# Cross attentions of a two-layer perceiver: the 257th probabilities sent through a DRAM row, transposes and copies two units at a time

## Chip, cores and metric

One core of one Trainium2 chip runs the whole program. The metric is the time of one execution on the device in microseconds. Engines run their own queues and meet at semaphores: PE (TensorE, matmuls; its weight loads, PEld, overlap them), DVE (VectorE), ACT (ScalarE), POOL (GpSimd), SP (SyncE, whose queue issues all the DMAs). PSUM has eight banks of 128 x 512 float32; only PE writes them by matmul, only DVE and ACT read them here.

## The reference, cut to what matters

64 sequences of 32 tokens of width 256 go through two layers. Each layer has a cross attention to a context of 257 positions per sequence, a self attention of its own kind, and a feed-forward part. The change touches only the two cross attentions, `_L0_xattn_ref` (4 key heads, with a mask and RMS norms) and the cross part of `_L1_xattn_ref` (8 key heads, LayerNorms):

```
q = norm(project(x)).reshape(16 heads, 128)
k = norm(ctx @ Wk)              # 257 positions, 4 or 8 key heads
v = ctx @ Wv
probs = softmax(q . k)          # 257 probabilities for each query row
out = (probs @ v) @ Wo
```

The kernel computes `probs @ v` as `(probs @ ctx) @ Wv`: first each query row's weighted sum of the 257 context rows, then the value projection of it.

## The kernel before

`cross_attention` runs once for each layer. A tile is four sequences (BT = 4 batches b = 0 to 3, 128 token rows), and there are 16 tiles. A batch has 32 tokens x 16 heads = 512 query rows, in four units (v = 0 to 3) of 128 rows each: `pr[:, v, :]` holds a unit's 128 x 257 scores and then probabilities, one query row to a partition.

Each engine walks the same schedule written out by hand: `tile` calls `slot(i, s, ...)` for s = 0 to 3. Slot s projects the keys of batch s and computes its scores, and handles batch s-1 (`back(i, s, 1, ...)`) and, in layer 0, the values of batch s-2. Work on the next tile's tokens and queries is spread over the slots: in slot 0 the tokens of tile i+1 are normalised, transposed on PE after the second key (L320) and their queries projected. `run` repeats `tile` in a loop; after the last tile, slots without keys drain what is left. Layer 1 takes the values of two batches together (`project_value_pair`, in slots 1 and 3).

PE's order in a slot: for g = 0 to 3 the key projection g (L345, two accumulating matmuls of 128x128 by 128x257, each run as two instructions) into one of two banks, then the transposition of unit g of batch s-1; in layer 1 key 4; then values (L391, or L403 in layer 1); the sum of the keys' squares over a head (L353); the scores of units 0 and 1 (L364); pieces of query or output work, with keys 5 to 7 of layer 1 among them; the scores of units 2 and 3; last, `weigh_context` for batch s-1 (L382), whose two halves go to banks PC0 and PC1.

`transpose_probs` transposes a unit's probabilities into bank PTb: positions 0 to 127 and 128 to 255 by two transposes (L373), and the 257th position by a third (L375), whose source is that one column broadcast over 128 columns; so its result holds, on every partition, the 128 rows' 257th probability. `copy_probs` on DVE (L861) copies the three blocks (128x384) into `pT[:, :, v*128:...]`. There is one bank PTb, so the transposes of unit v+1 wait for the copy of unit v (`pt_copied`), and each copy waits for its transposes (`pt_done`). `weigh_context` multiplies the first 256 context rows `cn` with `pT[:, 0:2]`, and DVE's `copy_weighed` (L869) adds the 257th position when it empties the bank: `pT[:, 2, :]` (the probabilities) times `cT[:, b, h, 256]` (that position's context value on this partition) plus the bank, into `pcT`.

In layer 0 ACT takes each key from its bank (L595) and squares it (L597). In layer 1 DVE takes it (`copy_key`, L826) and then ACT squares it (L591). The next key in that bank waits for the square (`k_sq`). ACT then makes the reciprocal root of the summed squares (L604, L606), DVE scales the scores into `pr` (`shift_scores`, L844 in layer 0, L836 in layer 1), ACT exponentiates (L611) and normalises (`norm_probs`, L617, signal `pn_done`), with `norm_probs` of unit 3 at the start of the next slot. `shift_scores` of unit v waits until the previous batch's unit v has been transposed, as it overwrites it.

DVE's order at a slot's start: (in slot 0) statistics of the next tokens, the reciprocal of unit 3's sum, `copy_weighed` of batch s-2's second half, then for each g `copy_key` g (layer 1) and `copy_probs` g; in slot 0 `norm_tokens` (L769) behind g = 0 and, in layer 1, `quantise_tokens` behind g = 2. `copy_weighed` of batch s-1's first half is the last thing in a slot.

SP loads the context of batch b (`load_context`, L294 and L296: cT 257 KB, cn 256 KB) for the next tile when `pcT` of this tile's batch b has been written.

Of the kernel before, what the change touches and what calls it, by code (L numbers as in the profile page):

```python
# [6 lines left out]
F32 = mybir.dt.float32  # L7
# [8 lines left out]
P = 128  # L16
H = 256
HC = H // P
# [77 lines left out]
def cross_attention(nc, d, X, Yc, ident, layer, tiles):  # L96
# [24 lines left out]
    with Part(nc) as ctx:  # L121
# [8 lines left out]

        wq = sb("wq", [P, HC, NH * HD])
# [42 lines left out]
        pT = sb("pT", [P, KC + 1, UNITS * P])  # L174
# [59 lines left out]
        pt_done = sig("probs_transposed", BT * UNITS)  # L234
        pt_copied = sig("pT_copied", BT * UNITS)
# [42 lines left out]
        def _(sp):  # L278
# [10 lines left out]
            for s in ctx_in:  # L289
                s.prime(sp)  # L290

# [6 lines left out]

            load_context(0, 0)
# [4 lines left out]
            with sp.Fori(1, tiles) as i:  # L304
                for b in range(BT):
                    load_context(i, b)
# [4 lines left out]
        def _(pe):  # L311
# [56 lines left out]
            def transpose_probs(t, b, v):  # L368
                u = UNITS * b + v
                pe.wait_ge(pn_done.sem, pn_done.now(t, u + 1))  # L370
                pe.wait_ge(pt_copied.sem, pt_copied.after(t, u))
                for c in range(KC):
                    pe.transpose(PTb[:, c * P:(c + 1) * P], pr[:, v, c * P:(c + 1) * P], ident[:])  # L373
                last = pr[:, v, LAST:SE].to_broadcast([P, P])
                pe.transpose(PTb[:, KC * P:(KC + 1) * P], last, ident[:]).then_inc(pt_done.sem, 1)  # L375

            def weigh_context(t, b):
                pe.wait_ge(pt_copied.sem, pt_copied.now(t, UNITS * (b + 1)))
# [99 lines left out]
            def slot(i, s, cur, prev, nxt):  # L478
                for g in range(4):
                    if cur:  # L480
                        project_key(i, s, g)
                    for t, b in back(i, s, 1, cur, prev):
                        transpose_probs(t, b, g)
                    if g == 1 and s == 0 and nxt:
                        if prev:
                            pe.wait_ge(pc_copied.sem, pc_copied.now(i - 1, HC * (BT - 1)))
                        transpose_tokens(i + 1)
# [230 lines left out]
        def _(dve):  # L718
# [110 lines left out]
            def shift_scores(t, b, v):  # L829
# [3 lines left out]
                dve.wait_ge(pt_done.sem, pt_done.after(t, u + 1 - UNITS))  # L833
# [22 lines left out]
            def copy_probs(t, b, v):  # L856
                dve.wait_ge(pt_done.sem, pt_done.now(t, UNITS * b + v + 1))
                if v == 0:
# [89 lines left out]
            def slot(i, s, cur, prev, nxt):  # L948
# [6 lines left out]
                for g in range(4):  # L955
                    if L1 and cur:
                        copy_key(i, s, g)
                    for t, b in back(i, s, 1, cur, prev):
                        copy_probs(t, b, g)
# [1768 lines left out]
```

## Time and profile before

| | |
|---|---|
| median of 3 runs | 4377.0 us (4372.99 to 4379.25) |
| profiled execution | 4376.91 us, its span 4375.1 us |
| instructions | 84534 |
| PE busy | 3906.8 us, 89% |
| PE weight loads busy | 2551.8 us, 58% |
| DVE busy | 2551.3 us, 58% |
| ACT busy | 1863.2 us, 43% |
| POOL busy | 216.3 us, 5% |

The cross attention of layer 0 lies roughly in the second to tenth of the page's 40 slices, that of layer 1 in slices 22 to 35. Matmuls are pipelined: the time of one (283 ns on average for a transpose) is longer than the distance from its start to the next one's start, so the distances between starts in the timeline tell what one costs. A line of the timeline merges equal instructions that follow each other (x4 is four). "[0.70 <-PE ...]" is the engine's idle time before the line and what ended it.

### The profile page before, as it was taken

What the parts mean: (1) busy time and instruction counts of PE and PEld (TensorE: products, weight loads), DVE (VectorE), ACT (ScalarE), POOL (GpSimd) and SP (SyncE); (2) the same over time, 40 slices, a digit from 0 to 9 for tenths busy, and PEclk for the clock granted to TensorE, in tenths of its full rate; (3) what the DMA queues carried; (4) which work ended last, traced back from release to release, by engine and by line L of the source; (5) the groups of instructions that cost most, each with busy time, mean ns of one, the idle gap of its engine ahead of it and who ended that gap; (6) DMA issues with size and microseconds to landing.
All of it is one profiled execution on the core that took longest, in us unless ns stands there. A gap on an engine that the chain in (4) does not pass through costs nothing. (4 is left out here: it accounts for less than half of the span.)

```text
span 4375.1 us, 84534 instructions
## 1 busy us (share of the span) xinstructions
PE 3906.8 (89%) x29984; PEld 2551.8 (58%) x29984; DVE 2551.3 (58%) x6013; ACT 1863.2 (43%) x5062; POOL 216.3 (5%) x164
## 2 busy tenths in 40 slices
PE   6999999999799985888874999999999999789798
PEld 3666666666433552555553666666666666579555
DVE  4565655555311445777764677776777667457521
ACT  4555555555365113344432444444444444223111
POOL 0000000000000000222220000000000000000000
PEclk9999999999899987899886999999999999888799
DMA  3100100101000001000002000000000000000000
GB/s 108 34 29 29 34 29 29 34 29 34 34 1 33 0 0 58 1 0 0 0 1 78 25 24 24 24 24 24 24 23 20 24 24 24 25 6 0 32 0 19
DMA packets 90644, 105.19 MB, mean 24 GB/s; under 512 B 6320, under 2 KB 85808, under 8 KB 89136
## 3 DMA queue, kind: packets, MB, share of 16 engines
q1 hardware_dynamic: 90544, 103.86, 7.4%
q8 instruction: 63, 1.03, 0.1%
q14 instruction: 37, 0.30, 0.0%
HBM read 101.74 MB, written 2.10 MB: 24 GB/s over the span
## 5 line engine op out<-in xcount | busy, mean ns | idle before, releaser
L345 PE MATMUL x_Kb<-x_cT,x_wk 128*128 128x257 f32 x3072 | 801.9, 385 | 34.4 <-ACT x_sq L591 32.6
L345 PEld LDWEIGHTS x_Kb<-x_cT,x_wk 128*128 128x128 f32 x3072 | 542.3, 191 | 194.0 <-issue 93.6
L382 PE MATMUL x_PC<-x_pT,x_cn 128*128 128x512 f32 x1024 | 476.5, 608 | 2.5 <-DVE x_oT L879 0.8
L611 ACT ACTIVATE x_pr<-x_pr,x_ntop 128x257 f32<-128x257 f32 x512 | 261.0, 510 | 327.4 <-DVE x_ntop L841 186.6
L861 DVE COPY x_pT<-x_PTb 128x384 f32<-128x384 f32 x512 | 283.8, 554 | 167.3 <-PE x_PTb L375 164.2
L591 ACT ACTIVATE x_sq<-x_Kb 128x257 f32<-128x257 f32 x512 | 195.3, 381 | 309.3 <-DVE x_kT L826 303.3
L382 PEld LDWEIGHTS x_PC<-x_pT,x_cn 128*128 128x128 f32 x1024 | 185.2, 191 | 241.9 <-issue 228.3
L826 DVE TENSOR_SCALAR x_kT<-x_Kb,x_vecs 128x257 f32<-128x257 f32 x512 | 247.1, 483 | 133.9 <-PE x_Kb L345 129.8
L364 PE MATMUL x_Sb<-x_kT,x_qT 128*32 128x257 f32 (+1 forms) x4096 | 275.5, 383 | 5.0 <-DVE x_pr L844 3.4
L617 ACT ACTIVATE x_pr<-x_pr,x_rps 128x257 f32<-128x257 f32 x512 | 241.8, 500 | 82.1 <-DVE x_rps L854 81.3
L329 PE MATMUL x_PC<-x_wq,x_xnT 128*128 128x512 f32 x512 | 241.8, 607 | 4.4 <-DVE x_xnT L800 3.9
L411 PE MATMUL x_PC<-x_wo,x_oT 128*128 128x256 f32 x1024 | 235.6, 384 | 6.1 <-DVE x_oT L920 5.3
L1711 PE MATMUL c_B<-c_wqk,c_xq 128*128 128x512 f32 x384 | 196.4, 668 | 43.6 <-DVE c_qk L1977 31.5
L869 DVE SCALAR_TENSOR_TENSOR x_pcT<-x_pT,x_cT,x_PC 128x512 f32<-128x512 f32 x256 | 190.5, 745 | 72.7 <-PE x_PC L382 69.0
L373 PE MATMUL x_PTb<-ident,x_pr 128*128 128x128 f32 x1024 | 205.8, 283 | 25.7 <-DVE x_pT L861 22.6
L411 PEld LDWEIGHTS x_PC<-x_wo,x_oT 128*128 128x128 f32 x1024 | 193.9, 192 | 38.5 <-issue 6.2
L373 PEld LDWEIGHTS x_PTb<-ident,x_pr 128*128 128x128 f32 x1024 | 115.7, 141 | 141.4 <-issue 119.3
L704 POOL COPY x_qT<-x_qTn 128x512 f32<-128x512 f32 x128 | 77.7, 651 | 2385.1 <-ACT x_qTn L582 1356.2
L364 PEld LDWEIGHTS x_Sb<-x_kT,x_qT 128*32 128x32 f32 x4096 | 125.8, 110 | 117.6 <-issue 45.9
L836 DVE CUSTOM_DVE_ANT_0 x_pr<-x_Sb,x_rs 128x257 f32<-128x257 f32 x256 | 108.8, 425 | 129.8 <-ACT x_rs L606 121.5
L595 ACT ACTIVATE x_kT<-x_Kb,x_bkv 128x257 f32<-128x257 f32 x256 | 121.9, 476 | 128.1 <-PE x_Kb L345 117.9
L1711 PEld LDWEIGHTS c_B<-c_wqk,c_xq 128*128 128x128 f32 x384 | 79.1, 212 | 147.8 <-issue 91.3
(285 smaller groups left out, 6537.9 us busy)
## 6 DMA issues: line engine op xcount, KB each, us to landing
x_cT<-in_ctxT SPq DMA_DIRECT2D x128, 257.0 KB, 2.8
x_cn<-in_ctx SPq DMA_DIRECT2D x128, 256.0 KB, 2.9
x_wq<-in_x_wq SPq DMA_DIRECT2D x2, 2048.0 KB, 7.6
x_wo<-in_x_wo SPq DMA_DIRECT2D x2, 2048.0 KB, 16.1
e_w<-in_e_w SPq DMA_DIRECT2D x3, 1152.0 KB, 7.7
c_wqk<-in_c_wqk SPq DMA_DIRECT2D x2, 1536.0 KB, 8.2
X<-in_x SPq DMA_DIRECT2D x1, 2048.0 KB, 8.1
c_wo<-in_c_wo SPq DMA_DIRECT2D x1, 2048.0 KB, 17.6
```

Of the source, the lines that this page charges most:

```text
L329: m = pe.matmul(QB[k][:, :], xnT[:, c, :], wq[:, c, k * 512:(k + 1) * 512], start=c == 0, stop=c == HC - 1)
L345: m = pe.matmul(Kb[j % 2][:, 0:SE], wk[:, c, g * HD:(g + 1) * HD], cT[:, b, c, :], start=c == 0, stop=c == HC - 1)
L364: m = pe.matmul(Sb[v % 2][a * S:(a + 1) * S, 0:KW], qT[:, b, J * g + j, :], kT[:, g, :], start=True, stop=True)
L373: pe.transpose(PTb[:, c * P:(c + 1) * P], pr[:, v, c * P:(c + 1) * P], ident[:])
L382: m = pe.matmul(PC[h][:, :], cn[:, b, c, h * P:(h + 1) * P], pT[:, c, :], start=c == 0, stop=c == KC - 1)
L411: m = pe.matmul(PC[1][:, 0:H], oT[:, h, :], wo[:, h, :], start=h == 0, stop=h == NH - 1)
L591: act.activation(sq[:, g, :], Kb[j % 2][:, 0:SE], ACT.Square).then_inc(k_sq.sem, 1)
L611: act.activation(pr[:, v, :], pr[:, v, :], ACT.Exp, bias=ntop[:, u:u + 1], scale=1.0 if L1 else -1.0, accum_out=ps[:, u:u + 1]).then_inc(e ...
L617: act.activation(pr[:, v, :], pr[:, v, :], ACT.Copy, scale=rps[:, u:u + 1]).then_inc(pn_done.sem, 1)
L826: dve.tensor_scalar(kT[:, g, 0:SE], Kb[j % 2][:, 0:SE], vecs[:, 8:9], None, ALU.mult).then_inc(k_raw.sem, 1)
L861: dve.tensor_copy(pT[:, :, v * P:(v + 1) * P], PTb[:, 0:(KC + 1) * P].rearrange("p (c r) -> p c r", r=P)).then_inc(pt_copied.sem, 1)
L1711: m = pe.matmul(banks[PB[k]][:, :], xq[:, kind * HC + c, :], w[:, c, :], start=c == 0, stop=c == HC - 1)
```

## The change

The third transpose goes. The 257th probabilities of a batch (512 of them, one element to a partition and unit in `pr`) are written by a DMA to a DRAM row `last_row[b % 2]`, and a second DMA reads that row back to all 128 partitions of a new tile `last[:, b % 2, :]`. `copy_weighed` takes them from there and waits for that DMA. Bank PTb then has room for two units (4 x 128 columns): `transpose_probs` and `copy_probs` handle two units at a time, p = 0 or 1, at g = 0 and g = 2. SP's program issues both DMAs of each batch among the context loads, and its last tile is written out apart. `shift_scores` of unit 0 also waits until the previous batch's send has landed.

```diff
+        last_row = nc.dram_tensor(n + "last_row", [2, UNITS * P], F32, kind="Internal").ap()
-        pT = sb("pT", [P, KC + 1, UNITS * P])
+        pT = sb("pT", [P, KC, UNITS * P])
+        last = sb("last", [P, 2, UNITS * P])
...
+            def send_last(i, b, nxt):
+                if not nxt:
+                    sp.wait_ge(last_back.sem, last_back.after(i, b - 1))
+                sp.wait_ge(pn_done.sem, pn_done.now(i, UNITS * (b + 1)))
+                sp.dma_start(last_row[b % 2].rearrange("(v r o) -> r v o", v=UNITS, o=1), pr[:, :, LAST:SE],
+                             allow_slow_non_contiguous=True).then_inc(last_sent.sem, 16)
+            def fetch_last(i, b, nxt):
+                if not nxt:
+                    sp.wait_ge(pc_copied.sem, pc_copied.after(i, HC * (b - 1)))
+                sp.wait_ge(last_sent.sem, last_sent.now(i, b + 1))
+                sp.dma_start(last[:, b % 2, :], last_row[b % 2].unsqueeze(0).to_broadcast([P, UNITS * P])
+                             ).then_inc(last_back.sem, 16)
+            def tile(i, first, nxt):
+                for b in range(BT):
+                    send_last(i, b, nxt)
+                    if b == 0 and not first:
+                        load_context(i, BT - 1)
+                    if b > 0 and nxt:
+                        load_context(i + 1, b - 1)
+                    fetch_last(i, b, nxt)
...
-            with sp.Fori(1, tiles) as i:
-                for b in range(BT):
-                    load_context(i, b)
+            tile(0, True, True)
+            with sp.Fori(1, tiles - 1) as i:
+                tile(i, False, True)
+            tile(tiles - 1, False, False)
...
-            def transpose_probs(t, b, v):
-                u = UNITS * b + v
-                pe.wait_ge(pn_done.sem, pn_done.now(t, u + 1))
-                pe.wait_ge(pt_copied.sem, pt_copied.after(t, u))
-                for c in range(KC):
-                    pe.transpose(PTb[:, c * P:(c + 1) * P], pr[:, v, c * P:(c + 1) * P], ident[:])
-                last = pr[:, v, LAST:SE].to_broadcast([P, P])
-                pe.transpose(PTb[:, KC * P:(KC + 1) * P], last, ident[:]).then_inc(pt_done.sem, 1)
+            def transpose_probs(t, b, p):
+                pe.wait_ge(pn_done.sem, pn_done.now(t, UNITS * b + 2 * p + 2))
+                pe.wait_ge(pt_copied.sem, pt_copied.after(t, 2 * b + p))
+                for v in range(2):
+                    for c in range(KC):
+                        at = v * KC + c
+                        m = pe.transpose(PTb[:, at * P:(at + 1) * P], pr[:, 2 * p + v, c * P:(c + 1) * P], ident[:])
+                m.then_inc(pt_done.sem, 1)
...
-                    for t, b in back(i, s, 1, cur, prev):
-                        transpose_probs(t, b, g)
+                    if g in (0, 2):
+                        for t, b in back(i, s, 1, cur, prev):
+                            transpose_probs(t, b, g // 2)
...
-                dve.wait_ge(pt_done.sem, pt_done.after(t, u + 1 - UNITS))
+                dve.wait_ge(pt_done.sem, pt_done.after(t, 2 * (b - 1) + v // 2 + 1))
+                if v == 0:
+                    dve.wait_ge(last_sent.sem, last_sent.after(t, b))
...
-            def copy_probs(t, b, v):
-                dve.wait_ge(pt_done.sem, pt_done.now(t, UNITS * b + v + 1))
+            def copy_probs(t, b, p):
+                dve.wait_ge(pt_done.sem, pt_done.now(t, 2 * b + p + 1))
...
-                dve.tensor_copy(pT[:, :, v * P:(v + 1) * P],
-                                PTb[:, 0:(KC + 1) * P].rearrange("p (c r) -> p c r", r=P)).then_inc(pt_copied.sem, 1)
+                dve.tensor_copy(pT[:, :, 2 * p * P:2 * (p + 1) * P].rearrange("k c (v r) -> k v c r", v=2),
+                                PTb[:, :].rearrange("k (v c r) -> k v c r", v=2, c=KC)).then_inc(pt_copied.sem, 1)
...
-                    dve.wait_ge(pt_copied.sem, pt_copied.now(t, UNITS * (b + 1)))
+                    dve.wait_ge(last_back.sem, last_back.now(t, b + 1))
...
-                dve.scalar_tensor_tensor(pcT[:, h, b % NPC, :], pT[:, KC, :], cT[:, b, h, LAST:SE], PC[h][:, :],
+                dve.scalar_tensor_tensor(pcT[:, h, b % NPC, :], last[:, b % 2, :], cT[:, b, h, LAST:SE], PC[h][:, :],
                                          ALU.mult, ALU.add).then_inc(pc_copied.sem, 1)
```

`copy_probs` is called at g = 0 and g = 2 on DVE in the same way.

## Rows read from the trace of the kernel before

**Rows 1.** Table of stages, the two cross attentions: length, busy time by engine, clock, DMA.

```profile
core 0: us, PE busy (x) PEld busy (x) DVE busy (x) ACT busy (x) POOL busy (x), PEclk, DMA share, GB/s
76.86:1120.17 1043.31, 1036.00 (x6585) 672.31 (x6584) 611.30 (x1634) 603.67 (x1557) 38.77 (x60) 1.00 0.10 30
2412.52:3762.92 1350.40, 1278.88 (x8033) 863.29 (x8032) 952.84 (x2442) 626.20 (x1684) 34.35 (x60) 1.00 0.08 24
```

**Rows 2.** Timeline, layer 0, slots 1 and 2: start, duration, engine, line.

```profile
606.50 1.03 PE L345 MATMUL x_Kb<-x_cT,x_wk 128*128 128x257 f32 x4
...
611.64 1.95 PE L391 MATMUL x_PC<-x_pcT,x_wv 128*128 128x128 f32 x16
...
627.61 1.03 PE L345 MATMUL x_Kb<-x_cT,x_wk 128*128 128x257 f32 x4
...
628.48 0.38 PE L373 MATMUL x_PTb<-ident,x_pr 128*128 128x128 f32 x2
...
628.81 1.03 PE L345 MATMUL x_Kb<-x_cT,x_wk 128*128 128x257 f32 x4
...
630.27 0.56 DVE L861 COPY x_pT<-x_PTb 128x384 f32<-128x384 f32 x1 [0.70 <-PE x_PTb L375]
...
632.59 1.95 PE L391 MATMUL x_PC<-x_pcT,x_wv 128*128 128x128 f32 x16
```

**Rows 3.** Groups by line: shape, count | busy us, mean ns | idle before.

```profile
L861 DVE COPY x_pT<-x_PTb 128x384 f32<-128x384 f32 x512 | 283.8, 554 | 167.3 <-PE x_PTb L375 164.2
...
L375 PE MATMUL x_PTb<-ident,x_pr 128*128 128x128 f32 x512 | 140.0, 273 | 0.0
...
L879 DVE TENSOR_TENSOR x_oT<-x_PC,x_bkv 128x512 f32<-128x512 f32 x64 | 44.3, 692 | 46.6 <-PE x_PC L391 45.4
```

**Rows 4.** Timeline, layer 0, slot 3 and the next tile's slot 0.

```profile
644.08 1.03 PE L345 MATMUL x_Kb<-x_cT,x_wk 128*128 128x257 f32 x4
...
657.76 0.73 DVE L869 SCALAR_TENSOR_TENSOR x_pcT<-x_pT,x_cT,x_PC 128x512 f32<-128x512 f32 x1
...
658.49 1.03 PE L345 MATMUL x_Kb<-x_cT,x_wk 128*128 128x257 f32 x4
...
660.60 0.41 DVE L769 TENSOR_SCALAR x_xn<-X,x_mv,x_lr 128x256 f32 x1
...
663.86 1.95 PE L391 MATMUL x_PC<-x_pcT,x_wv 128*128 128x128 f32 x16
...
667.50 0.43 DVE L844 SCALAR_TENSOR_TENSOR x_pr<-x_Sb,x_rs 128x257 f32<-128x257 f32 x1 [0.97 <-ACT x_rs L606]
```

**Rows 5.** Timeline, layer 1, slots 0, 1 and 2 of one tile.

```profile
2632.07 1.03 PE L345 MATMUL x_Kb<-x_cT,x_wk 128*128 128x257 f32 x4
...
2638.68 0.48 DVE L826 TENSOR_SCALAR x_kT<-x_Kb,x_vecs 128x257 f32<-128x257 f32 x1
...
2639.71 0.64 PE L353 MATMUL x_SSb<-x_sq,x_ones 128*32 128x257 f32 x8 [0.70 <-ACT x_sq L591]
...
2645.60 1.14 PE L345 MATMUL x_Kb<-x_cT,x_wk 128*128 128x257 f32 x4 [0.73 <-ACT x_sq L591]
...
2653.36 1.03 PE L345 MATMUL x_Kb<-x_cT,x_wk 128*128 128x257 f32 x4
...
2659.38 3.73 PE L403 MATMUL x_PC<-x_pcT,x_wv 128*128 128x128 f32 x32
...
2675.70 1.03 PE L345 MATMUL x_Kb<-x_cT,x_wk 128*128 128x257 f32 x4
...
2677.86 0.39 ACT L591 ACTIVATE x_sq<-x_Kb 128x257 f32<-128x257 f32 x1 [0.53 <-DVE x_kT L826]
...
2682.28 0.64 PE L353 MATMUL x_SSb<-x_sq,x_ones 128*32 128x257 f32 x8
```

**Rows 6.** DMA queue (packets, MB, share of 16 engines) and issues (count, KB, us to landing).

```profile
q1 hardware_dynamic: 90544, 103.86, 7.4%
...
x_cT<-in_ctxT SPq DMA_DIRECT2D x128, 257.0 KB, 2.8
...
out_x<-X SPq DMA_DIRECT2D x1, 2048.0 KB, 7.5
```

More of the change, by code:

```diff
@@ L233, in cross_attention @@
         pn_done = sig("probs_normed", BT * UNITS)
-        pt_done = sig("probs_transposed", BT * UNITS)
-        pt_copied = sig("pT_copied", BT * UNITS)
+        pt_done = sig("probs_transposed", BT * 2)
+        pt_copied = sig("pT_copied", BT * 2)
+        last_sent = sig("last_probs_sent", BT, 16)
+        last_back = sig("last_probs_back", BT, 16)
         pc_done = sig("pc_done", BT * HC)
@@ L290, in _ @@
                 s.prime(sp)
+            last_sent.prime(sp)
+            last_back.prime(sp)
             def load_context(i, b):
@@ L366, in scores @@
                 m.then_inc(s_done.sem, 1)
-            def transpose_probs(t, b, v):
-                u = UNITS * b + v
-                pe.wait_ge(pn_done.sem, pn_done.now(t, u + 1))
-                pe.wait_ge(pt_copied.sem, pt_copied.after(t, u))
-                for c in range(KC):
-                    pe.transpose(PTb[:, c * P:(c + 1) * P], pr[:, v, c * P:(c + 1) * P], ident[:])
-                last = pr[:, v, LAST:SE].to_broadcast([P, P])
-                pe.transpose(PTb[:, KC * P:(KC + 1) * P], last, ident[:]).then_inc(pt_done.sem, 1)
+            def transpose_probs(t, b, p):
[6 more added lines that the diff above has]
+                m.then_inc(pt_done.sem, 1)
             def weigh_context(t, b):
-                pe.wait_ge(pt_copied.sem, pt_copied.now(t, UNITS * (b + 1)))
+                pe.wait_ge(pt_copied.sem, pt_copied.now(t, 2 * (b + 1)))
                 pe.wait_ge(pc_copied.sem, pc_copied.after(t, HC * b))
@@ L854, in invert_sum @@
                 dve.reciprocal(rps[:, u:u + 1], ps[:, u:u + 1]).then_inc(r_done.sem, 1)
-            def copy_probs(t, b, v):
-                dve.wait_ge(pt_done.sem, pt_done.now(t, UNITS * b + v + 1))
-                if v == 0:
+            def copy_probs(t, b, p):
+                dve.wait_ge(pt_done.sem, pt_done.now(t, 2 * b + p + 1))
+                if p == 0:
                     dve.wait_ge(pc_done.sem, pc_done.after(t, HC * b))
                     dve.wait_ge(pc_copied.sem, pc_copied.after(t, HC * b))
-                dve.tensor_copy(pT[:, :, v * P:(v + 1) * P],
-                                PTb[:, 0:(KC + 1) * P].rearrange("p (c r) -> p c r", r=P)).then_inc(pt_copied.sem, 1)
+                dve.tensor_copy(pT[:, :, 2 * p * P:2 * (p + 1) * P].rearrange("k c (v r) -> k v c r", v=2),
+                                PTb[:, :].rearrange("k (v c r) -> k v c r", v=2, c=KC)).then_inc(pt_copied.sem, 1)
             def copy_weighed(t, b, h):
                 if h == 0:
-                    dve.wait_ge(pt_copied.sem, pt_copied.now(t, UNITS * (b + 1)))
+                    dve.wait_ge(last_back.sem, last_back.now(t, b + 1))
                     dve.wait_ge(v_done.sem, v_done.after(t, b // 2 * 2 if L1 else b))
                 dve.wait_ge(pc_done.sem, pc_done.now(t, HC * b + h + 1))
-                dve.scalar_tensor_tensor(pcT[:, h, b % NPC, :], pT[:, KC, :], cT[:, b, h, LAST:SE], PC[h][:, :],
+                dve.scalar_tensor_tensor(pcT[:, h, b % NPC, :], last[:, b % 2, :], cT[:, b, h, LAST:SE], PC[h][:, :],
                                          ALU.mult, ALU.add).then_inc(pc_copied.sem, 1)
@@ L957, in slot @@
                         copy_key(i, s, g)
-                    for t, b in back(i, s, 1, cur, prev):
-                        copy_probs(t, b, g)
+                    if g in (0, 2):
+                        for t, b in back(i, s, 1, cur, prev):
+                            copy_probs(t, b, g // 2)
                     if g == 0 and s == 0 and nxt:
```

## The prediction

> **What bounds the kernel now.** I read the slices of the page first, then the two attention stretches in the table of stages, then the timeline of single slots. The change touches only the two cross attentions, 1043 and 1350 of the 4375 us [rows 1]. In them TensorE is busy 1036 and 1279 us at a granted clock of 1.00 (its 2.4 GHz level); VectorE 611 and 953, ScalarE 604 and 626 [rows 1]. So TensorE sets the time, and only what shortens its queue, or a wait in it, counts.
>
> The work repeats by slots (one batch each, four to a tile, 16 tiles), and the timeline gives a slot's head in single steps. I write K for a key projection, T for a transposition, times from the slot's first K. In layer 0: K to T is 0.87, three T's take 0.33, so 0.11 each (their 273 ns overlap), and the values' matmuls start at 4.98 [rows 2]. Work alone would be 4 x 1.20 = 4.80. The rest is a loop: T's end, VectorE copies (0.56), the next T may write the one bank again. Copy plus idle before it is 0.56 + 0.70 = 1.26 [rows 2], over the 1.20 of TensorE's own work: in this stretch TensorE waits for the copy. In the slot that starts at 606.50 the head is 5.14 [rows 2], as the second T waits longer for a copy that began late.
>
> **The change, part by part.**
>
> *Transpositions.* The 512 one-column ones go [rows 3]: 4 x 0.11 = 0.44 us of a slot. The other 1024 remain.
>
> *Copies.* 512 of 128x384 at 554 ns [rows 3] become 256 of 128x512. Not in the trace in this form; below lies 0.554 (no longer than now), above the 0.73 of the two-input operation of this width that reads a bank [rows 4]; the nearest row is 128x512 from a bank at 0.692 [rows 3]. I take 0.69. VectorE loses 284 - 177 = 107 us of work, worth nothing by itself.
>
> *Order.* The head becomes K0, 4 T, K1, K2, 4 T, K3. With 0.87 a key and 0.44 for four T's, starts are: T01 0.87, K1 1.31, K2 2.18, T23 3.05, K3 3.52 (0.03 for the change of work after a K), end 4.39. T23 may write from copy's end on: last T at 1.20, copy from 1.51 to 2.20. So the loop that binds now has 0.85 us of slack. Behind K3 no transposition hides the squaring of its output, but in layer 0 the 1.9 us of values' matmuls do [rows 2].
>
> Layer 0, gain per slot: 5.14 - 4.39 = 0.75 in slot 1, 4.98 - 4.39 = 0.59 in slots 2 and 3. In slot 0 the next tile's tokens are transposed after K1. VectorE makes them right behind the first copy; now they are there at 660.60 + 0.41 - 658.49 = 2.52 [rows 4]. The wider copy ends 0.1 later, but begins 0.1 earlier (VectorE is free at 1.43), so 2.53, plus 0.15 to TensorE: 2.68. TensorE is there at 2.18 and waits 0.5. From there 0.22 + 0.87 + 0.47 + 0.87 gives 5.11 against 663.86 - 658.49 = 5.37 [rows 4]: gain 0.26.
>
> Layer 1 has eight keys and VectorE copies each before ScalarE squares it, so the head ends with K4. Slots 1 and 3: K4 ends at 4.39 + 0.87 = 5.26; now the values' pair starts at 2659.38 - 2653.36 = 6.02 [rows 5], and 0.10 earlier in slot 3, whose second T is not held up. Gains 0.76 and 0.66. Slot 2: VectorE comes late from the rounding of the heads, the square of K0 ends at 2677.86 + 0.39 - 2675.70 = 2.55 [rows 5], so K2 starts at 2.60 instead of 2.18, T23 at 3.47, K3 at 3.94. Its copy and square end at 5.92 and the sum of squares follows at 5.97: now 6.58 [rows 5]. Gain 0.61, with a new wait of 0.3 for K3's square that T of unit 3 covers today. Slot 0 is bound by VectorE: first copy, tokens' normalisation, two key copies, second copy, four quantising operations, K3's copy. Before K3's copy stand two copies of 0.69 where three of 0.56 stood, but the second begins 0.17 later (the wider first copy puts the tokens and K2 0.10 later, and four T's stand behind K2) and lasts 0.14 longer. So K3's copy, now at 2638.68 - 2632.07 = 6.61, comes at 6.9, and the sum of squares, now at 7.64 after a wait of 0.70, at 7.88 [rows 5]: 0.24 worse. Behind it one copy fewer stands ahead of the scores' scaling, which is 0.14 earlier, and TensorE's later wait of 0.73 for the square of K5 [rows 5] hangs on that. Net gain 0.14.
>
> Sum. Layer 0: 14 x 0.26 + 15 x (0.75 + 0.59 + 0.59) + 4 x 0.59 for the last tile, where no tokens follow = 34.9. Layer 1: 14 x 0.14 + 15 x (0.76 + 0.61 + 0.66) + 2.2 = 34.6. In each layer one last slot has no keys: three loops of 1.26 and 0.33 become one of 1.50 and 0.44: 2.2 each. Together 34.9 + 34.6 + 4.4 = 74 us.
>
> *The row through DRAM.* 128 times: 512 elements of 4 bytes out, 512 elements to each of 128 partitions (262 KB) back. It costs no engine time outside SyncE's queue and the DMA engines: 33.5 MB more beside 103.9 MB that take 7.4% of them [rows 6]. What may wait: VectorE's first scores operation of the next batch overwrites the probabilities and needs the send landed. Unit 3's probabilities are ready at about 1.3 in slot 0, around 0 in the others; that operation is at 667.50 - 658.49 = 9.0 [rows 4], so 7 us are allowed. The trace has no send of single elements. Below: the 2.8 of the context load less its data, about 2.0. Above: 7.5, the one store, 2 MB, to DRAM [rows 6]. If each element is a packet, 32 fall to an engine, at 7.4% x 4375 x 16 / 90544 = 57 ns each [rows 6] 1.8. I take 2.0 + 1.8 = 3.8, near the load. Even doubled to 7.6 it would be late by half a microsecond in slot 0 alone, some 8 us in all. Behind the send in SyncE's queue stand two context loads, which have three slots of time, and the fetch. The fetch is due where VectorE writes the weighted context, 657.76 - 644.08 = 13.7 in the shortest slot of all [rows 4], 0.6 earlier after the change. As long as a context load of the same size, 2.8 [rows 6], and issued at about 4 to 5, it lands at 8. Five us of cover, so both cost nothing. The bounds for the fetch are 2.8 and the one-engine case below.
>
> The Trainium skill speaks against this part: "DMA: Bandwidth & Descriptors", section Rules for kernel authors, has a non-contiguous last dimension make one descriptor per element, and its Specifications put a read-modify-write on transfers under 512 B. By it the send is 512 descriptors of 4 bytes; no row here shows one, so the size of that penalty is open.
>
> The profiled execution took 4376.9, as the median of the runs, 4377.0. So 4376.9 - 74 = 4303 us.
>
> **Rivals.** *Only the work goes.* If the pair stages bring new waits of their own as large as the loop's old ones (keys back to back on two banks, the tokens' wait, K3's bare square), what is left is 128 x 0.44 = 56 us: 4321; with another 0.15 per slot lost, 4340. For it: layer 1's slots 0 and 2 are already bound by VectorE. Against: layer 0's slots show no wait but the copy's.
>
> *More than the head.* VectorE's 107 us also free layer 1's later waits (ScalarE's squares waiting for VectorE's key copies). If slots 0 and 2 gain 0.5 more each: 16 us, 4287.
>
> *The fetch is late.* All 128 rows read the same 2 KB of DRAM. Were it served by one engine's rate, the 262 KB would take 262 / 20 GB/s (103.9 MB over 7.4% of the 16 engines' span) = 13.1 us beside the 2.0. From an issue at 3.5 (4.8 in slot 0) it lands at 18.6 (19.9). Due in layer 0: 13.1 (slot 3), 15.1 (slot 2, 2.1 us longer), 15.9 (slot 0). Late by 5.5 + 3.5 + 4.0, less 1 us of cover each = 10 per tile; slot 1 (21.1 us) and layer 1's slots are long enough. 15.5 x 10 = 155: 4458, slower. It turns from gain to loss at a fetch of about 13.4 us. Against: the destination has 128 partitions like the context's, which lands in 2.8.
>
> The Trainium skill's section Rules for kernel authors of the same page, row Use all 16 engines, warns that a leading zero-stride dimension bounds the number of engines; with 128 copies it divides by 16, so by the rule all 16 serve it.
>
> **How the numbers follow.** Forecast 0.62 (4290 to 4315), only the work 0.19, more than the head 0.10, late DMA 0.09, of which a quarter, short of the full price, still ends faster or near no change. The range 4286 to 4338 leaves out the late DMA and the far end of the second. This kernel's change can be told from none at about 0.2% (9 us). Faster 0.91, same 0.02, slower 0.07.
>
> **What would show it.** The transposition group gone, 256 copies near 0.69; layer 0's values starting 4.4 after the first key in slots 1 to 3 and 5.1 in slot 0, where TensorE waits 0.5 for the tokens; layer 1's sum of squares at 7.9 in slot 0 and 6.0 in slot 2, there with a new wait for a square; no VectorE wait for a DMA. Wrong would be: waits on the sent or fetched row, a copy of 0.8 or more, or heads that shrink by less than 0.44.

## The result, and the profile after

The changed kernel took 4629.0 us (median of 4 runs, 4625.2 to 4644.9) beside 4378.1 for the kernel before: a ratio of 1.058, 95% interval 1.057 to 1.060. The forecast was 4303, in a range of 4286 to 4338, so it was slower by 251 us where 74 us of gain were foreseen.

The table of stages answers to [rows 1], over the same work (from the first key projection of the first tile's slot 2 to that of the last tile's slot 3):

```profile
core 0: us, PE busy (x) PEld busy (x) DVE busy (x) ACT busy (x) POOL busy (x), PEclk, DMA share, GB/s
83.25:1245.08 1161.83, 1035.81 (x6342) 673.38 (x6341) 563.89 (x1511) 602.66 (x1557) 37.38 (x60) 0.97 0.47 41
2536.41:4012.29 1475.88, 1298.73 (x7790) 881.85 (x7789) 911.26 (x2320) 624.95 (x1684) 34.24 (x60) 0.96 0.37 33
```

The stretches grew from 1043 to 1162 and from 1350 to 1476 us, 119 and 125. TensorE is idle for 126 and 177 us of them (7 and 72 before), and part of its busy time is run at the lower of its two clock levels after a wait. The DMA engines' share rose from 0.10 to 0.47 and from 0.08 to 0.37, while they move only 41 and 33 GB/s in place of 30 and 24.

The timeline of a slot 2 of layer 0, which answers to the one at 627.61 in [rows 2] (SPq is SyncE issuing a DMA; L377 is a key projection, L406 a transposition of probabilities, L423 the values):

```profile
619.68 0.37 SPq L310 DMA_DIRECT2D x_last_row<-x_pr  x1
619.73 1.03 PE L377 MATMUL x_Kb<-x_cT,x_wk 128*128 128x257 f32 x4
620.60 0.60 PE L406 MATMUL x_PTb<-ident,x_pr 128*128 128x128 f32 x4
621.03 1.90 PE L377 MATMUL x_Kb<-x_cT,x_wk 128*128 128x257 f32 x8
...
624.08 1.95 PE L423 MATMUL x_PC<-x_pcT,x_wv 128*128 128x128 f32 x16
...
627.17 0.42 ACT L639 ACTIVATE x_rs<-x_rs 128x257 f32<-128x257 f32 x1
...
631.10 0.34 SPq L318 DMA_DIRECT2D x_last<-x_last_row  x1
631.10 0.43 DVE L879 SCALAR_TENSOR_TENSOR x_pr<-x_Sb,x_rs 128x257 f32<-128x257 f32 x1 [4.35 <-DMA x_last_row<-x_pr]
...
631.68 0.64 PE L396 MATMUL x_Sb<-x_kT,x_qT 128*32 128x257 f32 x8 [0.58 <-DVE x_pr L879]
```

The head is what was foreseen: 624.08 - 619.73 = 4.35 (4.39 forecast, 4.98 before). Then, in the same slot, VectorE stands idle for 4.35 us ahead of its first operation on the new scores, which waits for the 512 single elements of the send. Not all of that is the send's: the operation also needs the keys' reciprocal roots, which ScalarE finished at 627.17 + 0.42 = 627.59. The send was issued at 619.68, so 7.9 us were allowed; it landed after 11.4, which is 3.5 late. SyncE's fetch, which waits for the same thing, goes out in that instant. TensorE then waits for VectorE.

From the groups, the DMA queues and issues, and VectorE's waits (us in total, times, longest):

```profile
L896 DVE COPY x_pT<-x_PTb 128x512 f32<-128x512 f32 x256 | 176.7, 690 | 137.0 <-PE x_PTb L406 135.8
...
q1 hardware_dynamic: 176560, 137.69, 26.2%
q14 instruction: 103, 0.84, 0.1%
...
x_last<-x_last_row SPq DMA_DIRECT2D x128, 256.0 KB, 4.7
...
DVE x_pr L879 <- DMA x_last_row<-x_pr: 196.7, 61, 6.8
DVE x_pr L871 <- DMA x_last_row<-x_pr: 99.5, 33, 6.0
DVE x_mv L797 <- issue: 24.3, 13, 2.1
DVE x_pcT L904 <- DMA x_last<-x_last_row: 19.3, 6, 10.0
DVE x_stats L794 <- issue: 18.3, 13, 1.6
```

The copy is 690 ns (0.69 taken). The waits for the send are 296 us in 94 places, of which a part, as in the slot above, would have been waited anyhow. The data queue went from 90544 packets and 7.4% [rows 6] to 176560 and 26.2%: 86016 more packets, 65536 of them the send's elements. But it is not these that fill the engines. In the trace's packet records an element of 4 bytes takes 8 ns, all of them together 0.8% of the engines' span; what grew are the packets of the context loads, which are issued just behind the sends: those of 1028 bytes (cT) from 60 to 320 ns on average, those of 1024 (mostly cn) from 48 to 108, together from 6.0% to 21.0%. So the time of the sends shows in the landing, and the share shows what they hold up. And two things are there that no wait of before answers to: the instruction queue, 37 packets before, moves 103; and VectorE's first operations of a tile wait, 13 times each, for nothing that the profile can name ("issue").

### The profile page after: what moved, and what is told of

It reads as the page before. It is cut to its first block and busy times, and to the rows that moved or that the text cites. A ratio compares the mean times of both kernels' runs of the same rounds, so it can differ in the third digit from the quotient of the medians.

```text
span 4623.6 us, 83474 instructions
## 1 busy us (share of the span) xinstructions
PE 3899.3 (84%) x29472; PEld 2547.7 (55%) x29472; DVE 2459.4 (53%) x5757; ACT 1858.5 (40%) x5062; POOL 214.7 (5%) x164
## 3 DMA queue, kind: packets, MB, share of 16 engines
q1 hardware_dynamic: 176560, 137.69, 26.2%
## 5 line engine op out<-in xcount | busy, mean ns | idle before, releaser
L377 PE MATMUL x_Kb<-x_cT,x_wk 128*128 128x257 f32 x3072 | 815.9, 399 | 62.2 <-ACT x_sq L624 59.0
L377 PEld LDWEIGHTS x_Kb<-x_cT,x_wk 128*128 128x128 f32 x3072 | 570.2, 199 | 252.4 <-issue 100.3
L414 PE MATMUL x_PC<-x_pT,x_cn 128*128 128x512 f32 x1024 | 494.6, 627 | 45.0 <-DVE x_qn L843 41.2
L396 PE MATMUL x_Sb<-x_kT,x_qT 128*32 128x257 f32 (+1 forms) x4096 | 285.2, 391 | 55.2 <-DVE x_pr L879 55.0
L896 DVE COPY x_pT<-x_PTb 128x512 f32<-128x512 f32 x256 | 176.7, 690 | 137.0 <-PE x_PTb L406 135.8
L904 DVE SCALAR_TENSOR_TENSOR x_pcT<-x_last,x_cT,x_PC 128x512 f32<-128x512 f32 x256 | 190.1, 744 | 106.6 <-PE x_PC L414 86.0
L879 DVE SCALAR_TENSOR_TENSOR x_pr<-x_Sb,x_rs 128x257 f32<-128x257 f32 x256 | 108.1, 422 | 222.1 <-DMA x_last_row<-x_pr 196.7
L637 ACT ACTIVATE x_rs<-x_SSb,x_eps_h 128x257 f32<-128x257 f32 x192 | 90.8, 473 | 190.3 <-PE x_SSb L385 181.5
L368 PE MATMUL x_PC<-ident,x_qn 128*128 128x128 f32 x512 | 88.3, 301 | 91.7 <-DVE x_qn L852 88.3
```

The costliest lines, as they stand in the source:

```text
L377: m = pe.matmul(Kb[j % 2][:, 0:SE], wk[:, c, g * HD:(g + 1) * HD], cT[:, b, c, :], start=c == 0, stop=c == HC - 1)
L396: m = pe.matmul(Sb[v % 2][a * S:(a + 1) * S, 0:KW], qT[:, b, J * g + j, :], kT[:, g, :], start=True, stop=True)
L896: dve.tensor_copy(pT[:, :, 2 * p * P:2 * (p + 1) * P].rearrange("k c (v r) -> k v c r", v=2), PTb[:, :].rearrange("k (v c r) -> k v c r", ...
L904: dve.scalar_tensor_tensor(pcT[:, h, b % NPC, :], last[:, b % 2, :], cT[:, b, h, LAST:SE], PC[h][:, :], ALU.mult, ALU.add).then_inc(pc_cop ...
```

## The experiments

Slot lengths below are distances in the timeline from a slot's first key projection to the next slot's, medians over 14 tiles. Before: 16.86, 21.12, 16.47 and 14.42 in layer 0 (slots 0 to 3), 21.30, 22.33, 23.59 and 21.95 in layer 1. "Send" is from its issue to the issue of the fetch, which waits for it. For 120 of the 128 sends the two context loads are issued in between, and SyncE's own issues then take 1.2 us or more of it; behind eight sends (the first, and three in the last tile, of each layer) stands no load. The cuts of code show the line that matters; the waits that go with it are left out. The runs e3 to e8 have the pairs and so, besides what they test, the cost that is found in e9 to e11.

### The two halves of the change apart

**e1_pairs_no_row.** The new order and copies; the row is a constant tile.

```
-                    send_last(i, b, nxt)
-                    fetch_last(i, b, nxt)
-                    dve.wait_ge(last_sent.sem, ...)   # and last_back's
+            dve.memset(last[:], 1.0 / 257)
```

> The changed kernel without both DMAs of the row and without the waits on them; the tile of 257th probabilities is set once to a constant, so that position's share of the output is left out. Theory S (all of the loss is the send of 512 single elements, which takes about 10 us to land and holds up the scores of the next batch; the pair stages gain what was predicted): 4303, within 10. Rival P (the pair stages lose time of their own, by keys back to back on two banks and wider copies): above 4378.

Measured: 4315.0 us, ratio 0.986 (0.985 to 0.988). Layer 0's slots are 16.86, 20.30, 15.93 and 13.79; layer 1's 21.54, 23.13 and 21.25 in slots 1 to 3, but slot 0 went up to 22.60. So the pairs save time, and one slot goes against them; the time is 2 us above the expected range.

**e2_before_plus_row.** The kernel before, with both DMAs and their waits; what comes back is not used.

```
+                    send_last(i, b, nxt)
+                    fetch_last(i, b, nxt)
+                    dve.wait_ge(last_sent.sem, last_sent.after(t, b))
+                    dve.wait_ge(last_back.sem, last_back.now(t, b + 1))
```

> The kernel before, with its third transposes and copies unit by unit, plus both DMAs of the row and the two waits on them; nothing uses what they bring. Theory S: the scores start when the send has landed, and the send starts when the probabilities are ready, so a shorter or longer head makes no difference where the wait binds: 4640 to 4690, near the changed kernel's 4629 and not 74 above it. Rival P: 4378 to 4420, the row costs little by itself. Rival C (the extra DMA traffic slows everything a little, the wait matters less): about 4700.

Measured: 4587.4 us, ratio 1.048 (1.046 to 1.050), VectorE waits 152.9 + 82.3 us for the send. The loss comes with the DMAs, with or without the pairs. It lies between the ranges of theory S (from 4640) and rival P (to 4420): the DMAs cost 211 us here and 314 beside the pairs (4629.0 - 4315.0). That is what theory S has in it: where the send binds, a shorter head gains nothing.

### What is slow in the send

**e3_quarter_send.** 128 of the 512 elements (one unit's; the rest of the row is fixed data).

```
+ sp.dma_start(last_row[b % 2][0:P].rearrange("(v r o) -> r v o", v=1, o=1), pr[:, 0:1, LAST:SE], ...)
```

> The changed kernel with only unit 0's 128 elements sent; the other three units' 257th probabilities are left out (the row holds fixed values there). Theory S with a cost by packet: 128 packets land in 2 + 8/4 = about 4 us, no wait binds: 4303 to 4310. Rival F (a fixed delay of any send of such elements to DRAM, near 9 us): 4580 to 4630.

Measured: 4432.8 us, ratio 1.012 (1.010 to 1.014). A quarter of the elements still takes 8.4 us (median; 7.1 to 11.3), where all take 10.1 (8.6 to 12.4) in the changed kernel: the time is not in proportion to their number, and the total lies between theory S and rival F.

**e4_side_tile.** ScalarE copies the four columns to a small tile, and 512 elements go out from there; VectorE need not wait for the send.

```
+ act.activation(side[:, b % 2, :].unsqueeze(2), pr[:, :, LAST:SE], ACT.Copy)
+ sp.dma_start(last_row[b % 2]..., side[:, b % 2, :].unsqueeze(2), ...)
```

> The changed kernel, but ScalarE first copies the four columns (128x4) to a tile of two buffers, and the send reads from there, still 512 single elements. The scores wait only for that copy. Theory S: the send still takes 10 us, the fetch lands at about 15.5 after the slot's first key, late by 1 to 2 us only in layer 0's shorter slots: 4330 to 4370. Rival C (traffic): stays near 4600.

Measured: 4469.7 us, ratio 1.022 (1.020 to 1.024). The wait for the send is gone, and the row's return is late in its place (80.0 us in 39 waits). The send itself is 10.1 us (median) as in the changed kernel: from which of the two tiles it reads does not matter. The total lies between the two theories' numbers.

**e5_packed_rows.** As e4, with the row laid out so that a partition's four values are neighbours: 128 packets of 16 bytes.

```
+ sp.dma_start(last_row[b % 2].rearrange("(r v) -> r v", v=UNITS), side[:, b % 2, :])
```

> As the side tile kernel, but the DRAM row is laid out by query row, so that a partition's four values are one run: 128 packets of 16 bytes instead of 512 of 4; VectorE reads the fetched tile with a stride of four. Theory L (single-element writes that share a line of DRAM hold each other up): the send lands in 3 to 5 us, no wait on the fetch: 4315 to 4335. Rival W (every small write to DRAM takes a fixed 7 to 8 us): the send lands in 7 to 8, the fetch just in time: 4325 to 4360. The trace's send time tells them apart more than the total.

Measured: 4399.1 us, ratio 1.005 (1.004 to 1.007), above both ranges; send 1.8 us. No wait for a send or fetch is left. It is 37 us slower than e6 below, and one difference is on record, VectorE's `copy_weighed`, which here reads the fetched row with a stride of four (this run, then e6):

```profile
L913 DVE SCALAR_TENSOR_TENSOR x_pcT<-x_last,x_cT,x_PC 128x512 f32<-128x512 f32 x256 | 291.7, 1142 | 50.2 <-PE x_PC L416 49.5
...
L920 DVE SCALAR_TENSOR_TENSOR x_pcT<-x_last,x_cT,x_PC 128x512 f32<-128x512 f32 x256 | 190.0, 743 | 76.1 <-PE x_PC L422 72.4 <-DMA x_last<-x_last_row 3.0
```

1.14 us in place of 0.74, 256 times. That this is all of the 37 us was not tested.

**e6_four_rows.** TensorE turns the four columns into four rows, ScalarE copies them, and four packets of 512 bytes go out.

```
+ pe.transpose(SSb[0:UNITS, 3 * P:4 * P], pr[:, :, LAST:SE].rearrange("p v o -> p (v o)"), ident[:])
+ act.activation(turned[:, b % 2, :], SSb[0:UNITS, 3 * P:4 * P], ACT.Copy)
+ sp.dma_start(last_row[b % 2].rearrange("(v r) -> v r", v=UNITS), turned[:, b % 2, :])
```

> The changed kernel, but TensorE transposes the four columns at once (128x4 to 4x128, one transpose behind the second pair's, into a free part of the squares' bank), ScalarE copies 4x128 out, and the send is 4 packets of 512 B. The scores wait only for that transpose. Cost: 0.11 to 0.2 us of TensorE and 0.3 us of ScalarE per batch. Theory L: send 2 to 2.5 us, total 4330 to 4345, faster than before. Rival W: send 7 to 8 us, fetch at 3.7 + 0.8 + 7.5 + 4.7 = 16.7 after the slot's first key, late in layer 0: 4390 to 4450.

Measured: 4362.5 us, ratio 0.997 (0.995 to 0.998); send 1.6 us. The total is over theory L's 4345 and under rival W's 4390.

**e7_spread_send.** 512 single elements as in the changed kernel, straight from the probabilities, but each 512 bytes from the next in DRAM. The fetch reads a fixed row, so the 257th probabilities are left out.

```
+ sp.dma_start(spread[b % 2].rearrange("(v r) o -> r v o", v=UNITS)[:, :, 0:1], pr[:, :, LAST:SE], ...)
```

> The changed kernel with the 512 elements sent to places 512 B apart; the fetch reads a row of fixed values, so the 257th probabilities are left out. Same number of packets, none share a line. Theory L: the send lands in 3.5 to 5 us, the scores do not wait: 4315 to 4330. Rival W: 9 to 12 us as before: 4600 to 4640.

Measured: 4364.9 us, ratio 0.997 (0.996 to 0.998); the send was faster than theory L's 3.5 to 5 us, the total 35 us over its range. The data queue's line, that of the send's issues and SyncE's issues in one slot, of this kernel:

```profile
q1 hardware_dynamic: 176624, 137.70, 10.9%
...
x_spread<-x_pr SPq DMA_DIRECT2D x128, 2.0 KB, 1.8
...
629.29 0.37 SPq L312 DMA_DIRECT2D x_spread<-x_pr  x1
...
631.48 0.36 SPq L320 DMA_DIRECT2D x_last<-x_last_row  x1
```

This is the run that decides. The packets are as many as in the changed kernel and as small; the fetch goes out 2.19 us after the send in place of 11.42, the context loads' packets are back at 68 and 48 ns, and the queue's share is 10.9% in place of 26.2%. Neither the number of packets nor their 4 bytes alone is the cost: it is that single elements are written to neighbouring places. By e5, neighbouring places do no such harm either when a packet holds 16 bytes.

Two other causes can be ruled out from sends that the traces already hold. The loads behind a send do not hold it up: the eight sends of the changed kernel without one took 8.6 to 11.6 us, those of this kernel 1.8 to 2.0. Nor does a fetch from the row that is being written: the changed kernel's very first send, ahead of any fetch, took 10.9.

**e8_distinct_rows.** e6, with each partition fetching a row of its own.

```
-   last_row[b % 2].unsqueeze(0).to_broadcast([P, UNITS * P])
+   d["wq"][0:P, 0:UNITS * P]
```

> As the kernel with four rows, but the fetch reads 128 different rows of a weight matrix, 2 KB each, instead of one row 128 times; the 257th probabilities are left out. Theory H (the 4.7 us of the fetch come from all packets reading the same 2 KB): the fetch lands in 2.8 us like a context load and the DMA share falls. Rival: 4.7 us whatever the rows. Total as in the kernel with four rows, within 10, where no wait is on the fetch.

The 257th probabilities are left out. Measured: 4360.4 us against e6's 4362.5, landing in 3.6 us in place of 3.8, where 2.8 or 4.7 was expected. That all partitions read one row costs nothing to speak of; the rival of the late fetch is out.

### Where the other 60 us are

e6 to e8 have hardly a wait for the row (one of 3.0 us in e6) and yet stand about 60 us over the forecast. It is layer 1's slot 0: 26.00 us in e6 and 26.24 in e7, before 21.30; their other slots are shorter than before's. The timeline of the changed kernel there shows the two unnamed waits, the tokens' late normalisation, and TensorE behind the gap of 4.25 us at a granted clock of 0.50, its 1.2 GHz level (the four matmuls of a key in 1.92 us, not 1.03):

```profile
2679.48 0.43 DVE L794 BATCH_NORM_STATS2 x_stats<-X 128x6 f32 x1 [1.41 <-issue]
2681.98 0.18 DVE L797 BATCH_NORM_AGGREGATE x_mv<-x_stats 128x2 f32<-128x6 f32 x1 [2.08 <-issue]
2683.89 0.40 DVE L802 TENSOR_SCALAR x_xn<-X,x_mv,x_lr 128x256 f32 x1
...
2684.35 0.67 PE L352 MATMUL x_PC<-ident,x_xn 128*128 128x128 f32 x2 [4.25 <-DVE x_xn L802]
2684.81 1.92 PE L377 MATMUL x_Kb<-x_cT,x_wk 128*128 128x257 f32 x4
```

These are the first instructions after the loop's jump, and all kernels with the pairs move 102 or 103 instruction packets where before and e2 move 37 to 39. The theory: VectorE's code is fetched again at each jump. The packet records bear it out: in the changed kernel's layer 1, three packets of 8 KB on that queue start 1.0, 3.5 and 6.0 us (medians) after VectorE jumps back, and two more later in the turn. That is five a turn in 13 turns, 65 of the 66 by which the kernels differ; in the kernel before the same loop has none. A loop's place, below, is the number of VectorE instructions that stand before it in the compiled program: 1493 in the kernel before, 1472 in the changed one, 1461 in e1, 1518 in e2 (whose loop is 337 long, that of before 326). The experiments move the loop by increments of an unread semaphore in VectorE's setup, and change nothing else:

```
+            if L1:
+                for _ in range(22):      # 107, 32, 21, 30, 70 in the others
+                    dve.sem_inc(gate, 1)
             dve.sem_inc(ready, 1)
```

**e9_four_rows_plus22** (on e6)

> The four-row kernel (4362.5 us) with 22 more increments of an otherwise unread semaphore in VectorE's setup of the second cross attention, ahead of its loop, and nothing else. In the VectorE program that moves the loop's first instruction from place 1471 to 1493, where the kernel before has it. Theory C (the second attention's slot with the tokens, which takes 26.0 us in place of 21.3, waits for VectorE's own code: the loop's code is fetched again at its jump because of where the loop lies): the slot is back at 20.6 to 21.5 us, the instruction queue moves about 38 packets in place of 103, and the time is 4362 - 14 x 4.5 = 4299, between 4290 and 4312. Rival O (the slot is longer because of the order of the work in it, the pairs of transposes and copies): nothing moves, 4358 to 4367. Rival N (the code is fetched because the loop is shorter than before's, 324 instructions against 326): nothing moves either, and the 103 packets stay.

**e10_before_plus107** (on the kernel before)

> The kernel before with 107 of the same increments at the same point, which puts its second attention's VectorE loop at place 1600. If the code is held in pieces of 8 KB (the instruction queue's packets are of that size: 0.84 MB in 103) and an instruction takes 64 bytes, 107 places further is the same place within a piece as 21 places back, that is 1472, where the changed kernel's loop lies. Theory C with that arithmetic: the slot with the tokens grows from 21.3 to about 26 us in the second attention, the instruction queue moves about 100 packets in place of 37, and the time is 4378 + 14 x 4.6 = 4442, between 4395 and 4450. Rivals O and N: 4374 to 4384, the queue stays at 37 or 38 packets. If the place matters but not with that period, anything between.

**e11_pairs_plus32** (on e1)

> The pairs alone (nothing goes out to DRAM or comes back; the row is a constant; 4315.0 us) with 32 such increments, which moves the same loop from place 1461 to 1493. Theory C: the slot with the tokens goes from 22.6 to 20.6 to 21.2 us, the instruction queue from 102 packets to about 38, the time to 4315 - 14 x 1.3 to 1.8 = 4292 to 4300. Rivals O and N: nothing moves, 4311 to 4319.

Measured: e9 4303.8 us, ratio 0.983 (0.982 to 0.985), slot 0 at 21.07, 38 packets. e10 4446.2 us, ratio 1.016 (1.015 to 1.018), slot 0 at 25.65, 104 packets. e11 4298.5 us, ratio 0.982 (0.981 to 0.984), slot 0 at 21.07, 37 packets. All three are as the theory had it (e10 near the top of its range). The loss is 4.4 us a turn in e10, 4.9 in e6 and 1.5 in e1. In e10 nothing but unread increments was added to the kernel before, and it shows the same picture (first two lines; the other two are e9 at the same point):

```profile
2739.83 0.43 DVE L764 BATCH_NORM_STATS2 x_stats<-X 128x6 f32 x1 [1.33 <-issue]
2742.06 0.18 DVE L767 BATCH_NORM_AGGREGATE x_mv<-x_stats 128x2 f32<-128x6 f32 x1 [1.80 <-issue]
```

```profile
2766.41 0.42 DVE L813 BATCH_NORM_STATS2 x_stats<-X 128x6 f32 x1
2766.98 0.18 DVE L816 BATCH_NORM_AGGREGATE x_mv<-x_stats 128x2 f32<-128x6 f32 x1 [0.16 <-DVE x_stats L813]
```

e9 does the whole computation and beats both kernels: 4303.8 us. That this is the forecast's 4303 is chance: it is another kernel, with 128 more transposes and without the send that was forecast.

**e16_before_plus30** and **e17_before_plus70** ask what decides it.

> The kernel before with its second attention's VectorE loop (326 instructions) at place 1523. Theory P: the code is held in pieces of 128 instructions (8 KB), and a loop that touches three keeps its code while one that touches four loses it. The runs so far put the piece's edge at 1473 to 1493 (the loops at 1493 and 1518 touch three, the one at 1472 four), so this loop ends 356 to 376 places behind an edge, within three pieces (384): no loss, 4372 to 4384, 37 or 38 packets on the instruction queue. Rival R (only places just behind an edge are good): a loss, up to 4442 and 104 packets.

> The same with the loop at place 1563. Theory P: it ends 396 to 416 places behind an edge and so touches four pieces: the loss, 4425 to 4450, about 100 packets. If pieces of 16 KB (256 instructions), two of them held, decided it, this place would be as good as 1493 (326 and up to 90 are under 512): 4372 to 4384, 37 packets.

Measured: e16 4376.5 us, ratio 1.000 (0.999 to 1.001), 38 packets. e17 4420.6 us, ratio 1.010 (1.007 to 1.013), 103 packets, slot 0 at 23.95. Both go the way of theory P; e17 lost less than its range had (4425 to 4450), by two executions only. Its third packet starts 12.5 us after the jump, where it is 6.0 in e10 and 6.7 in e1, so the fetches are not held up alike in all of them. With one edge and pieces of 128 instructions, the loops at 1493, 1518 and 1523 touch three pieces and those at 1461, 1472, 1563 and 1600 four, and only the latter lose (the edge can lie anywhere from 1473 to 1493).

The Trainium skill, "Runtime: NRT & Kernel Launch", section Instruction fetch mechanics, has a taken branch whose target is not in the current window stall for a fetch; these runs agree in kind (24.3 + 18.3 us of unnamed waits at the jump). It gives blocks of 16 KiB, 256 instructions, two of them held. Here a packet of VectorE's queue is 8 KB (0.84 MB in 103), and e10 and e17 lose at places that two blocks of 256 would hold; the measurement decides.

### Both causes in the changed kernel

**e12_after_plus21.** The changed kernel with its loop at 1493.

> The changed kernel (4629.0 us) with 21 such increments, which puts its second attention's VectorE loop at place 1493, as in the kernel before. By theory C the code's fetches go: instruction queue 103 to about 38 packets. Additive (the code and the send cost apart from each other): the slot with the tokens goes from 25.9 to about 21.1 us and the time to 4629 - 14 x 4.8 = 4562, between 4550 and 4575. Rival Q (the send's wait takes the place of the code's, since the send of the slot before and the row's return still end where they did): the slot stays over 23.5 us, the time between 4590 and 4625.

Measured: 4648.8 us, ratio 1.062 (1.059 to 1.064). Neither. Slot 0 went from 25.9 to 22.6, but layer 0, whose code is the same, ended 37 us later: the sends took 10.8 us on average in place of 10.4. The two were measured apart, so both were run again, on one chip.

**e13_after_again**

> The changed kernel once more, as the partner of e14 on the same chip. If the length of the sends differs from chip to chip, it takes 4630 to 4680 here; sends of 10.3 to 10.9 us from issue to the fetch's issue. Rival: a chip makes no difference, 4620 to 4640.

**e14_after_plus21_b**

> The changed kernel with its second attention's VectorE loop at place 1493, on the same chip as e13. Additive: e13 less 14 x 3.4 to 4.8, that is 47 to 67 us less. Rival Q (the waits for the send take up what the code gives back): less than 30 us less. No difference at all would say that the code costs nothing while the sends are late.

**e15_spread_plus21** (on e7)

> The kernel whose 512 single elements go to places 512 B apart (4364.9 us; the row that is fetched is a fixed one), with the second attention's loop at place 1493 by 21 increments. If the two causes are all there is, it takes 4365 - 14 x 4.6 to 5.2 = 4292 to 4301, at or a little below the forecast of 4303 for the changed kernel; the slot with the tokens in the second attention 21.0 to 21.2 us. If something else of the change costs time, over 4310.

Measured, all on one chip, before at 4375.4: e13 4614.2 (ratio 1.055, 1.053 to 1.057), e14 4574.9 (1.046, 1.044 to 1.048), e15 4291.0 (0.981, 0.980 to 0.983). e13 lay below its expected 4630 and below the 4629 of the first measurement, with sends of 10.3 us on average. Code: 4614.2 - 4574.9 = 39 us, between "additive" (47 to 67) and rival Q (under 30): part of what it gives back goes into waits for the send, which are 286.7 us in e13 and 299.0 in e14. Adjacent writes: 4574.9 - 4291.0 = 284 us, 2.2 us for each of 128 sends. What is left is the gain of the pairs, 84 us. This split holds in this order only: with the adjacent writes in place the pairs gain next to nothing (e14's 4574.9 beside e2's 4587.4, on another chip). e15 came out 1 us under its range of 4292 to 4301. The two attentions of e15 (as [rows 1]) and its queues:

```profile
78.55:1089.07 1010.52, 998.88 (x6341) 662.48 (x6340) 559.12 (x1512) 603.55 (x1557) 38.69 (x60) 1.00 0.18 47
2370.12:3687.18 1317.06, 1242.18 (x7789) 849.73 (x7788) 909.70 (x2320) 627.92 (x1684) 34.24 (x60) 1.00 0.13 36
...
q1 hardware_dynamic: 176624, 137.70, 11.2%
q14 instruction: 38, 0.31, 0.0%
```

1043.3 - 1010.5 = 32.8 and 1350.4 - 1317.1 = 33.3 us less over this work, at a full clock again, where the prediction had about 35 for each layer. Another 11 us lie between the two stretches (1281.1 for 1292.4 us). Layer 0's end has 4.4 of them, 47.0 in place of 51.4 us from its last first key to the next stage, where the prediction had 0.6 + 2.2; most of the others lie in stages that the change does not touch. The stretch after them, of which the change touches only the start, was 594 to 612 us long in the traces of before, e1, e6, e7, e9, e11 and e15, so the rest of the 84 is not to be put down to anything.

## Why the prediction was wrong, point by point

*What bounds the kernel.* Right: with both faults taken away TensorE is busy in 99% and 94% of the two stretches (99% and 95% before).

*Transpositions, copies, order.* Right but for two small terms. Head 4.35 in layer 0's slots 1 to 3 (4.39), copy 0.690. Slots 1 to 3 gain 0.82, 0.54 and 0.63 in layer 0 (0.75, 0.59, 0.59) and 0.79, 0.47 and 0.70 in layer 1 (0.76, 0.61, 0.66), by e15. Slot 0 gains 0.14 in layer 0 (0.26), where TensorE waits 0.35 for the tokens (0.5), and 0.22 in layer 1 (0.14): the sum of squares comes at 7.88, as worked out. In layer 1's slot 2, K2 starts at 2.60 as worked out, and the new wait for K3's square is there, 0.20 (0.3); but the sum of squares comes at 6.12 and not at 5.97, which is what that slot's gain lacks.

*The send.* This is the step that failed: "I take 2.0 + 1.8 = 3.8, near the load". The 7 us allowed were on the safe side in layer 0: from the send's issue to the first operation on the scores, e15, where nothing waits for the send, has 7.5 in slot 0 and 8.0 to 8.2 in the others. In layer 1 it has 6.8 in slot 2 and 9.1 or more in the rest, so it is there that 7.6 would have been late. The landing takes about 10 us (8.6 to 12.4 from its issue to the fetch's), beyond even the upper bound of 7.5. The 1.8 came from the mean time of a packet of before, 57 ns, and that is the mean of packets of about 1 KB. An element of 4 bytes has 8 ns in the records, and e7 shows a send of 512 of them landing in 2.2 us at most where their places lie apart: there even 3.8 was too much. Written side by side they hinder each other, in a way that no packet's own time shows, and the sentence "even doubled to 7.6 it would be late by half a microsecond in slot 0 alone" set a limit where there was none. The price of 284 us follows from it, in two forms: VectorE's wait before it overwrites the probabilities, and behind it the fetch, which starts when the send has landed and not "at about 4 to 5".

The prediction had named the rule of one descriptor per element ("DMA: Bandwidth & Descriptors" of the Trainium skill) and left its price open; the packets are there (65536 more), and e7 shows that they alone are not the price. With that price open, "even doubled" was no bound.

*The fetch.* Its own time was too small but harmless: 4.7 us in the changed kernel and 3.8 in e6 for 2.8 assumed, with five us of cover, and one shared row is as quick as 128 distinct ones. The rival *the fetch is late* gave slower for a reason that did not hold. No rival named what happened.

*No term at all* stood for the place of the code. The change makes layer 1's VectorE loop three instructions shorter and starts it 21 places earlier, which pushes it over one more 8 KB piece: 63 us of layer 1's stretch from e6 to e9 and 69 from e7 to e15, 39 in the changed kernel.

## What to carry to other kernels

Single elements gathered from many partitions into one compact row of DRAM are the dear way to write: turn them on TensorE first, or send several neighbours per partition, or leave room between them (each tried here in one form only), and give a producer and its fetch the sum of both landings. When a change that touches few instructions costs a fixed amount at each turn of a loop, look at the instruction queue's packets and at unnamed waits behind the jump, and shift the loop by a few idle instructions before blaming the order of the work.

## What the runs showed of the hardware that was not expected

- A send of 512 elements of 4 bytes from 128 partitions: about 10 us to neighbouring places, 2.2 to places 512 bytes apart, 1.8 as 128 packets of 16 bytes, 1.6 as four packets of 512 (the last three are upper bounds, since SyncE issues two loads ahead of the fetch; without a load in between they are 1.8 to 2.0, mostly 1.4 to 1.5, and 1.2). 128 single neighbouring elements still take 8.4. How far apart places must lie was not tried, nor why a quarter of the elements takes over three quarters of the time. One thing fits and was not tested: e3 and the changed kernel put equally many elements (128) into each 512 bytes of the row, e5 a quarter as many packets.
- Loads queued behind such a send suffer with it: their packets of 1028 bytes took 320 ns on average in place of 60, and the data queue's share rose from 7.4% to 26.2%, while the send's own elements are 0.8%.
- VectorE's loop of 315 to 337 instructions runs freely while it touches three pieces of 128 instructions, and loses 1.5 to 5 us a turn when it touches four; five packets of 8 KB more a turn, three of them within 6 to 13 us of the jump. Why e1 lost only 1.5 us a turn and e17 2.7 is open, as is whether the edge lies where these seven places put it for other programs.
- Kernels with the adjacent writes differed from one measurement to another far more than the others: 4629.0 and 4614.2 us for the changed kernel, 4648.8 and 4574.9 for e12 and e14, which are the same, with sends of 10.8 and 10.4 us on average; the medians of the kernel before stayed within 4 us. A difference of some 50 us between two such kernels says something only if both ran side by side.
